# Attention maxima of two heads in one VectorE operation, and eight PSUM banks shared out anew

## The chip, the cores and the metric

The kernel runs on one core of a Trainium2 chip. The metric is the device time of one execution in microseconds, the median of several. The core has five engines: TensorE (PE), VectorE (DVE), ScalarE (ACT), GpSimd (POOL) and SyncE (SP, which here only issues DMAs). PSUM holds 8 banks of 512 float32 columns for each of 128 partitions; PE writes its results there.

## The reference

Four blocks run one after the other on `x` of 16 batches x 128 tokens x 256 channels, each adding its output times a gate: a recurrence over time (WKV), a gated feed-forward network, an attention with 16 heads of 8 dimensions, and a mixture of 8 experts with a shared one. The change lies in the attention. In it, x of one batch is read as 128 channels x 256 positions:

```python
q = einsum('oc,bct->bot', Wq, target) + bq      # target: layernorm(x), source: the context
k = einsum('oc,bcs->bos', Wk, source) + bk
v = einsum('oc,bcs->bos', Wv, source) + bv
dot = einsum('bhdt,bhds->bhts', q, k) / sqrt(8)         # 16 heads, 256 x 256 scores each
dot = mask * dot - (1.0 - mask) * 1e6
amap = softmax(dot, axis=-1) * mask
out = einsum('bhts,bhds->bhdt', amap, v)
```

The inputs make scores large, so the softmax needs the maximum of each row.

## The kernel before, in words

The attention stage takes from about 155 to 387 us. Each head's scores are computed twice. First straight (line 1126, `score`): 256 positions t as two halves of 128 partitions by 256 positions s, which fills one bank; DVE takes the maximum over s (line 1259), two numbers a partition. The maxima of all 16 heads go through a transpose on PE (1213), a negation on ACT (1289), a split into three bf16 parts on POOL and a round trip through DRAM into rows of `QKA`, the operand of the scores. Then the scores are computed a second time, turned (line 1141, `score_T`): s on the partitions, t on the columns, two heads to a bank, with the negated maximum already in the sum. ACT takes the exponential of such a bank (1308), and PE multiplies with the values (1225, PV, four column groups of 32), accumulating in bank 6.

The loop over batches (`turns`) has 8 slots a batch, the same for each engine. In slot p of batch b PE does the scores of heads pair p of batch b+2 and the turned scores of slot p of batch b, woven together (`pe_both`): for each of two halves n, one straight matmul, one turned, one straight, one turned; the two kinds use different rows of the array where they can. Then it does the PV of the slot two before. In slot 0 the PV of the previous batch and the maxima's transpose follow; in slot 1 another PV comes first, and after it ACT copies bank 6 out (1313); PE turns the result in slots 3 (1234) and 5 (1241), and projects a later batch in slot 6 (633). DVE does two reductions a slot, and in slots 3, 4 and 5 a reciprocal (1267), the division (1274) and the addition to x (1282). ACT does two exponentials a slot, the copy in slot 1, and now and then a piece of another batch's projection (652, 662). 14 of 16 batches have both kinds of scores in the loop; the last two have only turned ones (`pe_scoresT`, `act_tail_exp`, the tail), and the first two batches' straight scores are done before the loop (`pe_scores`).

Each engine executes its instructions in order. Semaphores tie them: `a_s` counts banks of scores filled, `a_red` banks reduced, `a_st` turned banks filled, `a_exp` exponentials done. Straight scores use banks 0, 1, 2 by turns and turned ones 3, 4, 5. `score_bank` makes PE wait until the bank's last user has been reduced, and `turned_bank` until the exponential has read the bank; with three banks that is three heads, or three exponentials, back. The 16th head uses bank 1 (4 for turned scores) so that every batch starts alike. Banks 6 and 7 hold the values' sums and small transposes.

Of the kernel before, what the change touches and what calls it, by code (L numbers as in the profile page):

```python
# [8 lines left out]
ALU = mybir.AluOpType  # L9
ACT = mybir.ActivationFunctionType  # L10
AX = mybir.AxisListType
# [39 lines left out]
def flamingo_kernel(nc, x, ctx, mask, g_xattn, g_ffn, time_decay, time_first, gate_wT, up_wT, down_wT,  # L51
# [11 lines left out]
    with ExitStack() as keep:  # L63
# [161 lines left out]
        with ExitStack() as part:  # L225
# [135 lines left out]
            def later(count):  # L361

                return not isinstance(count, int) or count > 0
# [263 lines left out]
            def at(g, k, ahead):  # L627

                return g + (k + ahead) // GB, (k + ahead) % GB
# [433 lines left out]
            with ExitStack() as att:  # L1063
# [36 lines left out]
                a_mg = semp("a_mg")  # L1100

                SBK = [bank[0], bank[1]]
                THIRDS = [n % 3 for n in range(HEADS - 1)] + [1]
                SBK3, TBK3 = bank[0:3], bank[3:6]

                def last_use(n):

                    return max(m for m in range(-HEADS, n) if THIRDS[m % HEADS] == THIRDS[n])
                PVB, MISC = bank[6], bank[7]

                PT = HP[:, :, :].rearrange("p (a s q) (r t) -> p a s (q r) t", a=2, s=2, r=2)
# [25 lines left out]
                def score_T(pe, k, q, st, m, to=None):  # L1137
                    rows, h = rows_of(turned_head(q, m))
                    if to is None:
                        to = TBK3[THIRDS[turned_at(q, st, m // 2)]]  # L1140
                    return pe.matmul(to[:, (m % 2) * T:(m % 2 + 1) * T], QKA[rows, k, 1, h, st * P:(st + 1) * P],  # L1141
                                     QKA[rows, k, 0, h, :], start=True, stop=True)

                def turned_at(i, st, half):

                    return 2 * (2 * i + st) + 1 - half
# [6 lines left out]
                def score_bank(pe, g, k, n):  # L1153

                    score_filled(pe, g, k, n)
                    pe.wait_ge(a_red, HEADS * (GB * g + k) + last_use(n) + 1)

                def turned_bank(pe, g, k, i, st, half):

                    b, m = GB * g + k, turned_at(i, st, half)  # L1160
                    if m == 0:
                        pe.wait_ge(a_mx[k], 32 * (g + 1))
                    if later(HEADS * b + last_use(m) + 1):
                        pe.wait_ge(a_exp, HEADS * b + last_use(m) + 1)

                def pe_scores(pe, g, k, p, SBK):

# [28 lines left out]
                def pe_both(pe, to_score, to_turn, p):  # L1196


                    i, st = p // 2, p % 2
                    for n, half in ((2 * p, 1), (2 * p + 1, 0)):  # L1200
                        to = SBK3[THIRDS[n]]
                        if first(GB * to_turn[0] + to_turn[1]) and p == 0:
                            pe.wait_ge(s_x2, 1 + 2 * G3 + n + 1)
                        score_bank(pe, *to_score, n)
                        score(pe, to_score[1], n, 0, to)
                        turned_bank(pe, *to_turn, i, st, half)
                        score_T(pe, to_turn[1], i, st, 2 * half)
                        score(pe, to_score[1], n, 1, to).then_inc(a_s, 1)
                        score_T(pe, to_turn[1], i, st, 2 * half + 1).then_inc(a_st, 1)
# [40 lines left out]
                    pch.wait()  # L1250
                    pool.tensor_tensor(Z3[:], Z3[:], rstd3[:, bass.ds(b, 1)].broadcast_to([P, T]), ALU.mult).then_inc(a_z3, 1)

                def dve_reduce(dve, g, k, n, SBK=None):
                    b, par = GB * g + k, k % 2
                    if n == 0 and later(b - 1):
                        dve.wait_ge(a_mxT, b - 1)
                    dve.wait_ge(a_s, HEADS * b + n + 1)
                    src = SBK[(HEADS * b + n) % 3] if SBK else SBK3[THIRDS[n]]
                    dve.tensor_reduce(MX[:, par, head_of(n), :], src[:, :].rearrange("p (a s) -> p a s", a=2),  # L1259
                                      axis=AX.X, op=ALU.max).then_inc(a_red, 1)  # L1260

                yt = MISC[:, :].rearrange("p (x r) -> p x r", r=2 * HD)

# [36 lines left out]
                def act_exp(act, g, k, i, st):  # L1300
                    b = GB * g + k
                    n = 8 * b + 2 * i + st
                    for half in (1, 0):
                        m = turned_at(i, st, half)
                        act.wait_ge(a_st, HEADS * b + m + 1)
                        if half == 1 and later(n - 3):
                            act.wait_ge(a_pv, n - 3)
                        act.activation(PT[:, i % 2, st, 2 * half:2 * half + 2, :].rearrange("p j t -> p (j t)"),  # L1308
                                       TBK3[THIRDS[m]], ACT.Exp).then_inc(a_exp, 1)

                def act_av(act, b):
                    act.wait_ge(a_pv, 8 * b + 8)
# [82 lines left out]
                def there(b, ahead=0):  # L1395

                    return not isinstance(b, int) or 0 <= b + ahead < B
# [31 lines left out]
                with nc.Block() as block:  # L1429
# [199 lines left out]
                    @block.vector  # L1629
                    def _(dve):  # L1630
                        fch = Chain(dve, s_dvech, after_wkv[0])
                        ln4 = Chain(dve, m_ln)
                        ch = Chain(dve, a_dve)
                        ln3 = Chain(dve, s_ln3, after_ln3[0])

                        def reduces(b, lo, hi):
                            for h in range(lo, hi):
                                dve_reduce(dve, 0, b, h, PRO)

                        for i in range(NI):  # L1640
                            if i > 1:
                                reduces(0, 4 * (i - 2), 4 * (i - 2) + 2)
                            dve_h1(dve, fch, G3, i)
                            dve_h(dve, fch, G3, i)
                            if i > 1:
                                reduces(0, 4 * (i - 2) + 2, 4 * (i - 2) + 4)
                            if i == 0:
                                dve_z3(dve, AHEAD_V)
                                dve.tensor_scalar(maskG[:, :, :], maskT[:, :, :], tg[:, 1:2], None, ALU.mult).then_inc(a_mg, 1)
                            if i == 1:  # L1650
                                dve_stats3(dve, ln3, 2)
                        dve_z3(dve, AHEAD_Q)
                        reduces(1, 0, 16)
                        dve_x2(dve, G3, DB)
                        dve.wait_ge(a_mg, 1)

                        def slot(ch, g, k, p):
                            b = GB * g + k
                            if there(b, AHEAD_S):
                                dve_reduce(dve, *at(g, k, AHEAD_S), 2 * p)  # L1660
                            if there(b, AHEAD_S):
                                dve_reduce(dve, *at(g, k, AHEAD_S), 2 * p + 1)
                            if isinstance(b, int) and 8 * b + p in LAST_STATS:
                                dve_one_of_last(dve, ln3, LAST_STATS.index(8 * b + p))
                            if p == 3 and there(b, -1):
                                dve_sums(dve, ch, b - 1)
                            if p == 4 and there(b, -1):
                                dve_y(dve, ch, b - 1)
                            if p == 5 and there(b, -1):
                                dve_x3(dve, b - 1)  # L1670
                            for t in STAT4.get(tail(b, p), ()):
                                dve_statistics(ln4, tiles_of(t))
                            for t in NORM4.get(tail(b, p), ()):
                                dve_normalise(dve, tiles_of(t), t + 1)
                            if tail(b, p) == MOST4:
                                dve.wait_ge(a_x3, B - 1)
                                alone(dve)
                                dve_statistics(ln4, OTHERS)
                            if tail(b, p) == MOST4 + 1:
                                dve_normalise(dve, OTHERS, NG)  # L1680
                            if tail(b, p) == MOST4 + 2:
                                hidden_shared(Chain(dve, m_dve), 0, 0)
                            if tail(b, p) == MOST4 + 5:
                                dve.wait_ge(a_x3, B)
                                alone(dve)
                                dve_statistics(ln4, LAST)
                            if tail(b, p) in range(TURN4, TURN4 + 2 * G3):
                                dve_turn4(dve, *divmod(tail(b, p) - TURN4, 2), SBK[(tail(b, p) - TURN4) % 2])

                        turns(dve, slot, ch, a_dve, 1)  # L1690
# [477 lines left out]
```

## Time and profile before

| | us |
|---|---|
| median of 3 runs (lowest, highest) | 521.47 (521.08, 521.91) |
| the profiled execution | 522.43 |
| its span, first to last instruction | 520.7 |
| busy in the span: PE, DVE, ACT, POOL | 473.5, 379.4, 243.7, 229.9 |
| mean granted clock of PE | 0.996 |

The profile comes from one execution. PE's matmuls overlap, so its busy time is no measure of its work. L1259 is line 1259 of the kernel. "Idle before" is the time in which an engine stood still ahead of an instruction, with the instruction or DMA that released it; a wait for several things is put down to the last of them.

### The profile page before, as it was taken

What the parts mean: (1) busy time and instruction counts of PE and PEld (TensorE: products, weight loads), DVE (VectorE), ACT (ScalarE), POOL (GpSimd) and SP (SyncE); (2) the same over time, 40 slices, a digit from 0 to 9 for tenths busy, and PEclk for the clock granted to TensorE, in tenths of its full rate; (3) what the DMA queues carried; (4) which work ended last, traced back from release to release, by engine and by line L of the source; (5) the groups of instructions that cost most, each with busy time, mean ns of one, the idle gap of its engine ahead of it and who ended that gap; (6) DMA issues with size and microseconds to landing.
All of it is one profiled execution on the core that took longest, in us unless ns stands there. A gap on an engine that the chain in (4) does not pass through costs nothing. (4 is left out here: it accounts for less than half of the span.)

```text
span 520.7 us, 10383 instructions
## 1 busy us (share of the span) xinstructions
PE 473.5 (91%) x3384; PEld 259.2 (50%) x3384; DVE 379.4 (73%) x770; ACT 243.7 (47%) x461; POOL 229.9 (44%) x304
## 2 busy tenths in 40 slices
PE   2988999998989889999899999998999999999993
PEld 2653564753733533334334334333434746788882
DVE  4989879789668989999888999999645734333331
ACT  2742223221222068888788888878611001133331
POOL 3673224143438447666667667413010470042433
PEclk9999999999999999999999999999999999999998
DMA  7655800000255536556576565620004124468753
GB/s 241 204 167 124 147 18 0 1 1 1 62 144 146 137 88 172 138 145 166 144 198 158 151 174 152 153 47 6 3 4 162 52 102 156 132 155 211 185 116 40
DMA packets 67255, 59.95 MB, mean 115 GB/s; under 512 B 10048, under 2 KB 62256, under 8 KB 67216
## 3 DMA queue, kind: packets, MB, share of 16 engines
q1 hardware_dynamic: 63712, 55.24, 39.1%
q0 software_dynamic: 3072, 4.21, 4.8%
q8 instruction: 22, 0.36, 0.3%
q14 instruction: 17, 0.14, 0.1%
q10 hardware_dynamic: 432, 0.00, 0.0%
HBM read 38.90 MB, written 22.50 MB: 118 GB/s over the span
## 5 line engine op out<-in xcount | busy, mean ns | idle before, releaser
L1259 DVE TENSOR_REDUCE MX<-psum 128x2 f32<-128x512 f32 x256 | 161.2, 683 | 17.1 <-PE psum L1126 16.4
L1308 ACT ACTIVATE HP<-psum 128x512 f32<-128x512 f32 x224 | 120.8, 603 | 29.1 <-PE psum L1141 27.5
L1126 PE MATMUL psum<-QKA 60*128 60x256 bf16 x512 | 79.7, 273 | 14.4 <-DVE MX L1259 9.8
L1225 PE MATMUL psum<-HP,VP 128*32 128x256 f32 x1024 | 81.8, 391 | 0.2 <-issue 0.2
L1141 PE MATMUL psum<-QKA 60*128 60x256 bf16 x512 | 78.8, 273 | 2.1 <-DMA QKA<-max_scr 1.6
L566 PE MATMUL psum<-space_a,space_w 128*128 128x512 f32 x160 | 72.6, 600 | 3.5 <-DVE HP L593 2.1
L1126 PEld LDWEIGHTS psum<-QKA 60*128 60x128 bf16 x512 | 33.0, 94 | 70.5 <-DVE MX L1259 53.0
L1848 POOL DMA_INDIRECT out_x<-OE,to_u x16 | 25.0, 1564 | 62.3 <-ACT OE L1883 59.9
L579 ACT ACTIVATE space_a<-psum,hgs 128x512 f32<-128x512 f32 (+1 forms) x24 | 15.6, 650 | 72.0 <-PE psum L566 46.4
L566 PEld LDWEIGHTS psum<-space_a,space_w 128*128 128x128 f32 x160 | 29.0, 190 | 39.4 <-issue 32.3
L1971 PE MATMUL psum<-XT,WE 128*128 128x256 f32 (+1 forms) x192 | 44.0, 379 | 0.9 <-ACT XT L1867 0.9
L199 PE MATMUL psum<-space_a,wsh 128*128 128x512 f32 (+1 forms) x96 | 43.6, 598 | 0.3 <-PEq L1429 0.3
L606 PE MATMUL psum<-space_w,HP 128*128 128x256 f32 x160 | 37.9, 385 | 0.0
L1971 PEld LDWEIGHTS psum<-XT,WE 128*128 128x128 f32 (+1 forms) x192 | 34.3, 181 | 7.3 <-issue 1.1
L1141 PEld LDWEIGHTS psum<-QKA 60*128 60x128 bf16 x512 | 30.7, 94 | 7.8 <-issue 3.8
L1225 PEld LDWEIGHTS psum<-HP,VP 128*32 128x32 f32 x1024 | 20.2, 108 | 27.0 <-issue 15.4
L606 PEld LDWEIGHTS psum<-space_w,HP 128*128 128x128 f32 x160 | 29.4, 190 | 5.9 <-issue 2.4
L2119 DVE SCALAR_TENSOR_TENSOR KR<-KR,psum 128x256 f32<-128x256 f32 (+1 forms) x24 | 10.1, 420 | 30.0 <-ACT KR L1874 30.0
L684 POOL TENSOR_TENSOR QK<-QK,PARTS 128x512 f32<-128x512 f32 x16 | 18.5, 1159 | 20.2 <-ACT PARTS L662 20.2
L199 PEld LDWEIGHTS psum<-space_a,wsh 128*128 128x128 f32 (+1 forms) x96 | 16.6, 181 | 21.2 <-issue 21.1
L465 DVE RECIPROCAL DEN<-DEN 128x512 f32<-128x512 f32 x8 | 26.6, 3338 | 0.0
L1874 ACT ACTIVATE KR<-psum 128x256 f32<-128x256 f32 (+1 forms) x24 | 9.2, 383 | 36.8 <-PE psum L1971 36.8
(191 smaller groups left out, 737.6 us busy)
## 6 DMA issues: line engine op xcount, KB each, us to landing
QKA<-stack_scr SPq DMA_DIRECT2D x32, 480.0 KB, 4.7
stack_scr<-PARTS SPq DMA_DIRECT2D x32, 192.0 KB, 2.6
WE<-in_W SPq DMA_DIRECT2D x16, 352.0 KB
stack_scr<-PARTS SPq DMA_DIRECT2D x32, 128.0 KB, 2.1
XD<-dispatched SPq DMA_DIRECT2D x8, 258.0 KB, 3.8
X<-in_x SPq DMA_DIRECT2D x4, 512.0 KB, 5.7
CTX<-in_ctx SPq DMA_DIRECT2D x4, 512.0 KB, 7.9
MB<-in_mask SPq DMA_DIRECT2D x16, 128.0 KB, 3.1
```

The costliest lines, as they stand in the source:

```text
L199: last = pe.matmul(bank[2 * i + side][0:m, :], (wsh1, wsh3)[side][:, h, i * P:i * P + m], ZT4[:, h, bass.ds(GT * g, GT)], start=(h == 0), ...
L465: dve.reciprocal(DEN[:, h, :], DEN[:, h, :]).then_inc(s_rec, 1)
L566: last = pe.matmul(to[:, :], w[:, h, i * P:(i + 1) * P], ZT[:, h, :], start=(h == 0), stop=(h == 1))
L606: pe.matmul(to[f], HP[:, i, t * P:(t + 1) * P], dw[:, i, :], start=(i == 0), stop=False)
L684: pool.tensor_tensor(QK2 if r == 0 else part_of(2), QK2, part_of(r), ALU.subtract).then_inc(a_rest, 1)
L1126: return pe.matmul(to[:, tt * T:(tt + 1) * T], QKA[rows, k, 0, h, tt * P:(tt + 1) * P], QKA[rows, k, 1, h, :], start=True, stop=True)
L1141: return pe.matmul(to[:, (m % 2) * T:(m % 2 + 1) * T], QKA[rows, k, 1, h, st * P:(st + 1) * P], QKA[rows, k, 0, h, :], start=True, stop=True)
L1225: last = pe.matmul(PVB[32 * j:32 * j + 32, (m // 2) * T:(m // 2 + 1) * T], VP[:, k, st, turned_head(i, m), :], PT[:, i % 2, st, m, :], sta ...
L1259: dve.tensor_reduce(MX[:, par, head_of(n), :], src[:, :].rearrange("p (a s) -> p a s", a=2), axis=AX.X, op=ALU.max).then_inc(a_red, 1)
L1308: act.activation(PT[:, i % 2, st, 2 * half:2 * half + 2, :].rearrange("p j t -> p (j t)"), TBK3[THIRDS[m]], ACT.Exp).then_inc(a_exp, 1)
L1848: pool.indirect_dma_start(out=out_rows, out_offset=bass.IndirectOffsetOnAxis(ap=to_u[:, e, a:a + 1], axis=0), in_=OE[:, s, a, :], in_offse ...
L1971: last = pe.matmul(bank[i][0:m, lo:lo + CAP], w[:, s, h, i * P:i * P + m], XT[:, s, h, :], start=(h == 0), stop=(h == 1))
```

## The change

The two reductions of a slot become one over two neighbouring banks, 1,024 columns, which writes the maxima of both heads and adds 2 to `a_red`. It waits until both banks are filled. Straight scores now use four banks, 0 to 3, two a slot; PE waits once per slot, for the pair of two slots before. Turned scores use two banks, 4 and 5, by turns, so PE waits for the exponential two before the one that the bank is for. The stage ahead of the loop and the tail are as they were.

```diff
--- before.py
+++ after.py
@@ -1100,12 +1100,7 @@
                 a_mg = semp("a_mg")
 
                 SBK = [bank[0], bank[1]]
-                THIRDS = [n % 3 for n in range(HEADS - 1)] + [1]
-                SBK3, TBK3 = bank[0:3], bank[3:6]
-
-                def last_use(n):
-
-                    return max(m for m in range(-HEADS, n) if THIRDS[m % HEADS] == THIRDS[n])
+                SBK4, TBK2 = bank[0:4], bank[4:6]
                 PVB, MISC = bank[6], bank[7]
 
                 PT = HP[:, :, :].rearrange("p (a s q) (r t) -> p a s (q r) t", a=2, s=2, r=2)
@@ -1137,7 +1132,7 @@
                 def score_T(pe, k, q, st, m, to=None):
                     rows, h = rows_of(turned_head(q, m))
                     if to is None:
-                        to = TBK3[THIRDS[turned_at(q, st, m // 2)]]
+                        to = TBK2[turned_at(q, st, m // 2) % 2]
                     return pe.matmul(to[:, (m % 2) * T:(m % 2 + 1) * T], QKA[rows, k, 1, h, st * P:(st + 1) * P],
                                      QKA[rows, k, 0, h, :], start=True, stop=True)
 
@@ -1153,15 +1148,16 @@
                 def score_bank(pe, g, k, n):
 
                     score_filled(pe, g, k, n)
-                    pe.wait_ge(a_red, HEADS * (GB * g + k) + last_use(n) + 1)
+                    if n % 2 == 0:
+                        pe.wait_ge(a_red, HEADS * (GB * g + k) + n - 2)
 
                 def turned_bank(pe, g, k, i, st, half):
 
                     b, m = GB * g + k, turned_at(i, st, half)
                     if m == 0:
                         pe.wait_ge(a_mx[k], 32 * (g + 1))
-                    if later(HEADS * b + last_use(m) + 1):
-                        pe.wait_ge(a_exp, HEADS * b + last_use(m) + 1)
+                    if later(HEADS * b + m - 1):
+                        pe.wait_ge(a_exp, HEADS * b + m - 1)
 
                 def pe_scores(pe, g, k, p, SBK):
 
@@ -1198,7 +1194,7 @@
 
                     i, st = p // 2, p % 2
                     for n, half in ((2 * p, 1), (2 * p + 1, 0)):
-                        to = SBK3[THIRDS[n]]
+                        to = SBK4[n % 4]
                         if first(GB * to_turn[0] + to_turn[1]) and p == 0:
                             pe.wait_ge(s_x2, 1 + 2 * G3 + n + 1)
                         score_bank(pe, *to_score, n)
@@ -1250,14 +1246,24 @@
                     pch.wait()
                     pool.tensor_tensor(Z3[:], Z3[:], rstd3[:, bass.ds(b, 1)].broadcast_to([P, T]), ALU.mult).then_inc(a_z3, 1)
 
-                def dve_reduce(dve, g, k, n, SBK=None):
+                def dve_reduce(dve, g, k, n, SBK):
                     b, par = GB * g + k, k % 2
                     if n == 0 and later(b - 1):
                         dve.wait_ge(a_mxT, b - 1)
                     dve.wait_ge(a_s, HEADS * b + n + 1)
-                    src = SBK[(HEADS * b + n) % 3] if SBK else SBK3[THIRDS[n]]
+                    src = SBK[(HEADS * b + n) % 3]
                     dve.tensor_reduce(MX[:, par, head_of(n), :], src[:, :].rearrange("p (a s) -> p a s", a=2),
                                       axis=AX.X, op=ALU.max).then_inc(a_red, 1)
+
+                def dve_reduce_pair(dve, g, k, p):
+                    b, par = GB * g + k, k % 2
+                    if p == 0:
+                        dve.wait_ge(a_mxT, b - 1)
+                    dve.wait_ge(a_s, HEADS * b + 2 * p + 2)
+                    lo = 2 * (p % 2) * 512
+                    dve.tensor_reduce(MX[:, par, p:p + HALF + 1:HALF, :],
+                                      psum[:, lo:lo + 1024].rearrange("p (h a s) -> p h a s", h=2, a=2),
+                                      axis=AX.X, op=ALU.max).then_inc(a_red, 2)
 
                 yt = MISC[:, :].rearrange("p (x r) -> p x r", r=2 * HD)
 
@@ -1306,7 +1312,7 @@
                         if half == 1 and later(n - 3):
                             act.wait_ge(a_pv, n - 3)
                         act.activation(PT[:, i % 2, st, 2 * half:2 * half + 2, :].rearrange("p j t -> p (j t)"),
-                                       TBK3[THIRDS[m]], ACT.Exp).then_inc(a_exp, 1)
+                                       TBK2[m % 2], ACT.Exp).then_inc(a_exp, 1)
 
                 def act_av(act, b):
                     act.wait_ge(a_pv, 8 * b + 8)
@@ -1657,9 +1663,7 @@
                         def slot(ch, g, k, p):
                             b = GB * g + k
                             if there(b, AHEAD_S):
-                                dve_reduce(dve, *at(g, k, AHEAD_S), 2 * p)
-                            if there(b, AHEAD_S):
-                                dve_reduce(dve, *at(g, k, AHEAD_S), 2 * p + 1)
+                                dve_reduce_pair(dve, *at(g, k, AHEAD_S), p)
                             if isinstance(b, int) and 8 * b + p in LAST_STATS:
                                 dve_one_of_last(dve, ln3, LAST_STATS.index(8 * b + p))
                             if p == 3 and there(b, -1):
```

## Rows read from the trace of the kernel before

**Rows 1.** Costliest groups of the page: busy us, mean ns | idle before, releaser (times).

```profile
L1259 DVE TENSOR_REDUCE MX<-psum 128x2 f32<-128x512 f32 x256 | 161.2, 683 | 17.1 <-PE psum L1126 16.4
...
L1308 ACT ACTIVATE HP<-psum 128x512 f32<-128x512 f32 x224 | 120.8, 603 | 29.1 <-PE psum L1141 27.5
...
L1126 PEld LDWEIGHTS psum<-QKA 60*128 60x128 bf16 x512 | 33.0, 94 | 70.5 <-DVE MX L1259 53.0
```

**Rows 2.** Table of waits from 199 to 357: us in total, times, longest.

```profile
PEld psum L1141 <- ACT HP L1297: 0.4, 1, 0.4
```

**Rows 3.** One batch: length; busy PE, PEld, DVE, ACT, POOL; granted clock; DMA share, GB/s.

```profile
306.92:318.75 11.83, 11.34 (x142) 4.51 (x139) 10.96 (x21) 10.42 (x22) 8.09 (x13) 1.00 0.66 174
```

**Rows 4.** Timeline in order of time, ACT: start us, us, instruction, [idle before <-releaser].

```profile
309.11 0.60 ACT L1313 ACTIVATE AV<-psum 128x512 f32<-128x512 f32 x1 [0.33 <-PE psum L1225]
...
309.61 2.06 ACT L1308 ACTIVATE HP<-psum 128x512 f32<-128x512 f32 x4
...
311.52 0.66 ACT L662 ACTIVATE PARTS<-QK 128x512 bf16<-128x512 f32 x1
...
313.38 1.09 ACT L1308 ACTIVATE HP<-psum 128x512 f32<-128x512 f32 x2 [0.23 <-PE psum L1141]
```

**Rows 5.** The same timeline, PE (PEld: weight loads).

```profile
308.19 0.28 PE L1213 MATMUL psum<-ident,MX 128*32 128x128 f32 x1
...
308.41 0.64 PE L1225 MATMUL psum<-HP,VP 128*32 128x256 f32 x8
...
308.98 0.28 PE L1126 MATMUL psum<-QKA 60*128 60x256 bf16 x1
...
310.15 0.09 PEld L1126 LDWEIGHTS psum<-QKA 60*128 60x128 bf16 x1 [0.62 <-DVE MX L1259]
...
310.57 0.64 PE L1225 MATMUL psum<-HP,VP 128*32 128x256 f32 x8
...
312.26 0.65 PE L1234 MATMUL psum<-ident,AV 128*128 128x128 f32 x4
...
312.97 0.37 PE L1141 MATMUL psum<-QKA 60*128 60x256 bf16 x2
...
315.13 0.44 PE L1241 MATMUL psum<-ident,YA 128*128 128x128 f32 x2
...
315.50 0.28 PE L1141 MATMUL psum<-QKA 60*128 60x256 bf16 x1
...
316.05 0.64 PE L1225 MATMUL psum<-HP,VP 128*32 128x256 f32 x8
...
316.73 0.69 PE L633 MATMUL psum<-Z,wq 128*128 128x256 f32 x2
...
317.36 0.28 PE L1126 MATMUL psum<-QKA 60*128 60x256 bf16 x1
```

**Rows 6.** The same, DVE, and one small reduction at 398 us.

```profile
309.40 3.68 DVE L1259 TENSOR_REDUCE MX<-psum 128x2 f32<-128x512 f32 x6 [0.77 <-PE psum L1126]
...
313.00 0.35 DVE L1267 RECIPROCAL RD<-psum 128x32 f32<-128x32 f32 x1
...
398.26 0.29 DVE L2026 TENSOR_REDUCE mxl<-L 128x16 f32<-128x128 f32 x1
```

**Rows 7.** Timeline, the tail's exponentials and PE's wait on one.

```profile
356.73 2.85 ACT L1297 ACTIVATE HP<-psum 128x1024 f32<-128x1024 f32 x3
...
357.80 0.12 PEld L1141 LDWEIGHTS psum<-QKA 60*128 60x128 bf16 x4 [0.71 <-ACT HP L1297]
```

**Rows 8.** Timeline, ACT's copies of the values, three of the 16.

```profile
199.40 0.60 ACT L1313 ACTIVATE AV<-psum 128x512 f32<-128x512 f32 x1 [0.33 <-PE psum L1225]
...
320.94 0.60 ACT L1313 ACTIVATE AV<-psum 128x512 f32<-128x512 f32 x1 [0.33 <-PE psum L1225]
...
356.24 0.60 ACT L1313 ACTIVATE AV<-psum 128x512 f32<-128x512 f32 x1
```

**Rows 9.** Timeline, a matmul of scores that waited for a DMA.

```profile
258.39 0.28 PE L1126 MATMUL psum<-QKA 60*128 60x256 bf16 x1 [0.86 <-DMA QKA<-stack_scr]
```

## What is predicted, before the changed kernel was run

> **What bounds the kernel now.** The costliest groups of the page come first [rows 1]: the maxima, 256 reductions of 161 us on DVE, and the exponentials, 224 of 121 us on ACT, both inside the attention loop. The weight loads of the scores' matmuls sat idle 53 us until DVE had freed a bank. In the table of waits, cut to the loop, the turned scores' matmuls have one wait on ACT, of 0.4 us, and that on L1297, the tail's [rows 2]. So three turned banks are enough for ACT today, and the three score banks are what stops PE. A batch of the loop takes 11.83 us, with DVE busy 10.96 and ACT 10.42 [rows 3]: both nearly full, ACT half a microsecond behind. The busy share of PE says little, since its matmuls overlap; their starts say more.
>
> So I read one batch, 306.92 to 318.75, start by start [rows 4 to 6]. PE's own work in a slot, without waits: the turned matmuls start in four steps 0.11 apart, the values' matmuls (PV) start about 0.53 after the first (315.50 to 316.05 is 0.55 with its rounding), and take 0.57 to the next thing (308.41 to 308.98): 1.10. Besides, once per batch: 0.22 for the maxima's transpose (308.19 to 308.41), 0.59 for L1234 (312.26 to 312.85, one step ahead of 312.97), 0.37 for L1241 (315.13 to 315.50), 0.73 for L633 with the gap before it (PV's end 316.62 to 317.36). Slots 1 and 2 follow each other without a PV, 0.44 for 0.53. 8 x 1.10 + 1.91 - 0.09 = 10.62. The other 1.21 of the 11.83 are waits; the largest is in slot 2, on DVE: PV starts there 1.59 after slot 1 (308.98 to 310.57) where 0.44 + 0.53 = 0.97 would do, so 0.62 [rows 5]. DVE idles 0.77 in slot 1, and then runs on [rows 6].
>
> **The change, part by part.** *Two reductions of 512 become one of 1,024*, in 14 batches x 8 slots = 112. Six back to back take 3.68 and one lasts 0.68, so they start 0.60 apart, 1.20 for a pair [rows 6]. A reduction of 128 elements lasts 0.29, one of 512 0.68 [rows 6]: 1.02 ns an element. The long one should last 0.68 + 0.52 = 1.20 and let the next start after 0.60 + 0.52 = 1.12: 0.08 saved. The ends: 0.15 saved, if only elements cost (1,024 x 1.02 ns = 1.05), and 0.08 lost, if the halves do not overlap at all (0.60 + 0.68 = 1.28). I take 0.08, as the slope is of the same operation. DVE's batch falls from 10.96 to 10.3.
>
> *The pair starts later*: it needs both heads, the second 0.22 after the first, so a DVE that waits restarts that much later. *Four score banks instead of three*: a slot now needs the pair of two slots back, whose banks are free some 1.25 after its start, itself 0.31 after that slot's last score. In the schedule below this stops PE nowhere. The counts that SP's fills and POOL's values wait for (L1363, L1329) keep their values and come with PE.
>
> *Two turned banks instead of three.* The matmul of turned bank m waits for exponential m-2 instead of m-3. It stands on PE's queue ahead of the second score of its head, the next head, and PV, so whatever it waits, DVE waits too. The trace has no such wait; its parts it has:
> a) with ACT free, an exponential starts 0.41 after the second turned matmul of its bank (312.97 to 313.38) [rows 4, 5];
> b) exponentials follow each other by (2.06 - 0.60)/3 = 0.49 [rows 4];
> c) in the tail one started at 356.73, lasted 1.02 (of three, 2.85 together), and PE's wait on it ended at 357.80, 0.05 after its end [rows 7]. So a bank is free 0.60 + 0.05, say 0.66, after its exponential's start;
> d) in slot 1 ACT first copies the values, 0.70 after the PV ahead of slot 1 started (308.41 to 309.11), and starts exponential 2 0.50 after that (309.61).
>
> Slot 2, counted from that PV: exponential 3 starts at 0.70 + 0.50 + 0.49 = 1.69, its bank is free at 2.35, slot 2's last matmul starts one step later at 2.46, the next PV at 2.66. Without waits this PV would start at 0.57 + 0.97 = 1.54, and it starts today at 2.16. The wait is 1.12 where the one on DVE was 0.62: 0.50 more.
>
> A slot that directly follows one in which ACT was empty: the exponentials start 0.52 and 1.01 after the first slot's start, the second bank is free at 1.67, and PE wants it at 1.10 + 0.22 = 1.32: a wait of 0.35. This strikes slots 5 and 0. Slots 4, 6, 7 and 1 have L1234, L1241, L633, and the transpose with the extra PV ahead of them, which cover it, but for 0.03 in slot 6; in slot 3, behind slot 2's long wait, 0.08 are left. ACT's other work (L662, L652, the negation) fits between. Waits: 1.12 + 0.08 + 0.35 + 0.03 + 0.35 = 1.93, and a batch 10.62 + 1.93 = 12.55, which is 0.72 more. With 10.3 of work in it DVE has 2 us to spare, so the price of the long reduction, anywhere between its ends, changes nothing.
>
> On grouping, the Trainium skill (Perfetto Trace Analysis, Optimizing Scalar/DVE Operations) says that a DVE operation on PSUM carries about 125 ns of overhead and that larger operations help where the engine is saturated; by that the estimated saving is 112 x 0.125 = 14 us, where the slope gives 9. The same section says that an engine that isn't saturated but makes others idle is better served by smaller pieces. No run here shows either yet; the second speaks against the change.
>
> **Sum.** The copies of the values start once per batch, 16 in all, among them at 199.40, 320.94 and 356.24 [rows 8]. The ten batches to 320.94 take 121.54; at 12.55 they take 125.5: +4.0. In one of them PE stood 0.86 in slot 0 for a DMA [rows 9], and more behind it; if the slower pace doesn't absorb such waits it is up to 1.6 more. I take +4.8. The three batches to 356.24 take 11.77 today; they have no L633 (-0.73), which uncovers slot 7 (0.35) and leaves 0.08 of slot 0's: 10.62 - 0.73 + 1.93 + 0.35 - 0.27 = 11.91, +0.14 each, +0.4. The loop's first batch, which copies no values, ends 0.4 later by the same walk (ACT starts empty, and the slots follow each other closely). Together +5.6. The tail and what follows are as before, and PE passes the delay on. The profiled execution took 522.43 with a span of 520.7, and the median of the runs is 521.47: 528.0 in the terms of the one, 527.1 in the other's.
>
> **The rivals.** 1, the other side: *turned banks come free before PE asks, and DVE's gain arrives.* What is left are waits on the pairs: 0.37 in slot 3 (pair 1 starts 0.64 after slot 1 does, its banks are free at 1.89 + 0.02, PE asks at 0.44 + 1.10 = 1.54) and some 0.29 ahead of L1241. 10.62 + 0.66 = 11.28, 0.55 less in 13 batches: -7, 514.3. For it: 53 us of waits on DVE and none on L1308 [rows 1, 2]. Against it: exponential 2 ended at 310.21 [rows 4], and PE would ask for its bank at 308.98 + 0.44 = 309.42. It decides where slot 2's wait stays under 0.1.
> 2: *the new waits fall into the old ones.* With 0.62 in slot 2 as today and 0.2 in slots 5 and 0, a batch takes 10.62 + 0.62 + 0.4 + 0.1 = 11.74: 521. For it: the waits of today are in the same slots. Against it: the chain in slot 2 would have to be 0.5 shorter, and each of its parts stands in a row.
> 3: *a reduction over two banks is dear.* DVE binds again where 8 of them and the other 10.96 - 9.60 = 1.36 fill 12.55, from 1.40 each. At 1.5 a batch is 13.4, 0.8 more in 13: 537. No row points to it.
>
> **Chances.** Forecast 0.60, rival 1 0.22, rival 2 0.12, rival 3 0.06. A measurement of this kernel tells 0.2%, 1 us, from nothing. Rival 2 spreads over that line, with 0.01 of it counted slower: faster 0.22, same 0.11, slower 0.67. If the batch's 0.72 is off by 0.3 either way the forecast alone is 523 to 530; for eight in ten it must take in part of rival 1: 516.5 to 530.
>
> **What the changed profile would show.** Right: weight loads of L1141 wait for L1308, 12 us or more, most of it in slot 2; the wait of L1126 on DVE under 15; copies of the values 12.5 apart; 112 reductions of 1.20, DVE busy some 9 less, and idle over 12 more in the loop. Wrong: copies 11.3 apart (rival 1), or a DVE without gaps at over 1.4 a reduction (rival 3). If the PV of slot 2 starts much before 2.66 after the PV ahead of slot 1, one of a to d is off.

## The result, and the profile after

| us | before | after |
|---|---|---|
| median | 521.28 (520.63 to 521.91) | 527.5 (526.84 to 527.56) |
| ratio, 95% interval | | 1.0116 (1.0095 to 1.0137) |
| the profiled execution | 522.43 | 527.45 |
| its span | 520.7 | 525.4 |
| DVE busy in the span | 379.4 | 376.3 |

One further execution of the changed kernel took 564.74 us at a granted clock of 0.851 and is left out of the range and the ratio; the median of the other three is 527.45. The forecast was 527.1. The costliest groups of the page after (the columns are those of [rows 1]; lines of the kernel have moved by a few, 1141 is now 1136, 1126 is 1121, 1225 is 1221, 1308 is 1314, 1313 is 1319):

```profile
L1264 DVE TENSOR_REDUCE MX<-psum 128x4 f32<-128x1024 f32 x112 | 136.1, 1220 | 21.8 <-PE psum L1121 20.7
...
L1314 ACT ACTIVATE HP<-psum 128x512 f32<-128x512 f32 x224 | 121.6, 598 | 33.1 <-PE psum L1136 32.4
...
L1136 PE MATMUL psum<-QKA 60*128 60x256 bf16 x512 | 82.3, 275 | 9.4 <-ACT HP L1314 7.3
...
L1121 PEld LDWEIGHTS psum<-QKA 60*128 60x128 bf16 x512 | 37.7, 94 | 48.0 <-issue 29.3
...
L1136 PEld LDWEIGHTS psum<-QKA 60*128 60x128 bf16 x512 | 30.4, 94 | 30.1 <-ACT HP L1314 22.0
```

The 112 long reductions last 1.22 each. The waits have changed places: the scores' weight loads waited 53 us for DVE before [rows 1], and now L1136, the turned scores, waits 22.0 for the exponentials by the row of the loads. The 7.3 of the matmuls' row are parts of the same stops, seen by the matmul instead of its weight load, and are not added. The table of waits of the loop alone, 199 to 364 us, says the same; before, L1141 had 0.4 there, on the tail's L1297 [rows 2]:

```profile
PEld psum L1136 <- ACT HP L1314: 20.9, 51, 0.8
...
DVE MX L1264 <- PE psum L1121: 19.0, 50, 0.8
...
PE psum L1136 <- ACT HP L1314: 7.3, 13, 0.6
...
PEld psum L1121 <- DVE MX L1264: 5.6, 13, 0.7
```

One batch of the changed kernel, in the timeline, with the PV ahead of slot 1 at its head (x2 or x4 behind an instruction means that so many follow each other in one row):

```profile
299.78 0.64 PE L1221 MATMUL psum<-HP,VP 128*32 128x256 f32 x8
...
300.49 0.60 ACT L1319 ACTIVATE AV<-psum 128x512 f32<-128x512 f32 x1 [0.33 <-PE psum L1221]
...
300.98 2.23 ACT L1314 ACTIVATE HP<-psum 128x512 f32<-128x512 f32 x4
...
301.07 1.23 DVE L1264 TENSOR_REDUCE MX<-psum 128x4 f32<-128x1024 f32 x1 [0.65 <-PE psum L1121]
...
301.62 0.09 PEld L1136 LDWEIGHTS psum<-QKA 60*128 60x128 bf16 x1 [0.84 <-ACT HP L1314]
...
302.12 0.09 PEld L1136 LDWEIGHTS psum<-QKA 60*128 60x128 bf16 x1 [0.27 <-ACT HP L1314]
...
302.44 0.64 PE L1221 MATMUL psum<-HP,VP 128*32 128x256 f32 x8
...
302.51 2.44 DVE L1264 TENSOR_REDUCE MX<-psum 128x4 f32<-128x1024 f32 x2 [0.22 <-PE psum L1121]
...
303.35 0.27 PE L1121 MATMUL psum<-QKA 60*128 60x256 bf16 x1
...
305.46 1.22 DVE L1264 TENSOR_REDUCE MX<-psum 128x4 f32<-128x1024 f32 x1 [0.25 <-PE psum L1121]
...
306.42 0.09 PEld L1136 LDWEIGHTS psum<-QKA 60*128 60x128 bf16 x1 [0.27 <-ACT HP L1314]
...
306.61 0.60 DVE L1280 SCALAR_TENSOR_TENSOR YA<-psum,maskG,RD 128x128 f32<-128x128 f32 x2
...
311.11 0.09 PEld L1136 LDWEIGHTS psum<-QKA 60*128 60x128 bf16 x1 [0.27 <-ACT HP L1314]
```

PV at 299.78, the copy of the values 0.71 later, exponential 2 1.20 later; slot 2's turned scores get their banks at 301.62 and 302.12, and the next PV starts at 302.44, which is 2.66 after the first. Before it was 2.16 [rows 5]. The waits at 306.42 and 311.11 are those of slots 5 and 0. DVE stands 0.65 ahead of slot 1's pair and 0.22 and 0.25 ahead of two later ones, where no idle time of over 0.15, the least that a row shows, stood between slot 1 and slot 7 before [rows 6]. The batch as a whole (columns as in [rows 3]) and three copies of the values [rows 8]:

```profile
300.35:312.79 12.44, 11.88 (x142) 5.02 (x139) 10.77 (x13) 10.44 (x21) 8.02 (x14) 1.00 0.59 157
```

```profile
200.30 0.60 ACT L1319 ACTIVATE AV<-psum 128x512 f32<-128x512 f32 x1 [0.33 <-PE psum L1221]
...
325.36 0.60 ACT L1319 ACTIVATE AV<-psum 128x512 f32<-128x512 f32 x1 [0.33 <-PE psum L1221]
...
361.05 0.60 ACT L1319 ACTIVATE AV<-psum 128x512 f32<-128x512 f32 x1
```

The steady batch takes 12.44 where it took 11.83, at nearly the same work of ACT (10.44) and slightly less busy time of DVE (10.77, 10.96 before). From copy to copy, ten batches take 125.06 (121.54 before), the three after them 35.69 (35.30), and the first copy comes 0.90 later: 4.81 together, and the span grew by 4.7. The medians differ by more, 6.2, since the profiled execution of the kernel before was 1.15 slower than its median and that of the changed kernel was not.

### The profile page after: what moved, and what is told of

It reads as the page before. It is cut to its first block and busy times, and to the rows that moved or that the text cites. A ratio compares the mean times of both kernels' runs of the same rounds, so it can differ in the third digit from the quotient of the medians.

```text
span 525.4 us, 10281 instructions
## 1 busy us (share of the span) xinstructions
PE 480.9 (92%) x3384; PEld 264.9 (50%) x3384; DVE 376.3 (72%) x658; ACT 244.1 (46%) x461; POOL 230.3 (44%) x304
## 5 line engine op out<-in xcount | busy, mean ns | idle before, releaser
L1264 DVE TENSOR_REDUCE MX<-psum 128x4 f32<-128x1024 f32 x112 | 136.1, 1220 | 21.8 <-PE psum L1121 20.7
L1136 PE MATMUL psum<-QKA 60*128 60x256 bf16 x512 | 82.3, 275 | 9.4 <-ACT HP L1314 7.3
L1121 PE MATMUL psum<-QKA 60*128 60x256 bf16 x512 | 85.2, 275 | 4.5 <-DVE MX L1255 1.5
L1121 PEld LDWEIGHTS psum<-QKA 60*128 60x128 bf16 x512 | 37.7, 94 | 48.0 <-issue 29.3
L1136 PEld LDWEIGHTS psum<-QKA 60*128 60x128 bf16 x512 | 30.4, 94 | 30.1 <-ACT HP L1314 22.0
```

The lines of the kernel that those rows point to most:

```text
L1121: return pe.matmul(to[:, tt * T:(tt + 1) * T], QKA[rows, k, 0, h, tt * P:(tt + 1) * P], QKA[rows, k, 1, h, :], start=True, stop=True)
L1264: dve.tensor_reduce(MX[:, par, p:p + HALF + 1:HALF, :], psum[:, lo:lo + 1024].rearrange("p (h a s) -> p h a s", h=2, a=2), axis=AX.X, op=A ...
```

## Experiments

Twelve more variants of the same loop (orders, bank shares, shortened exponentials) were timed, each in several executions against the kernel before on the same chip. The kernel before took 520.87 beside e1 to e4, 521.25 beside e5 to e8, 521.57 beside e9 to e11 and 523.17 beside e12, so runs of different groups are compared by their ratios. "Batch" is the steady distance of the copies of the values in each trace, 11.8 before and 12.44 after. The code excerpts are shortened.

| run | score/turned banks, reduction | us | ratio to before, 95% | batch |
|---|---|---|---|---|
| e1 | 4/2, single | 525.7 | 1.0099 (1.0079 to 1.0118) | 12.44 |
| e2 | 3/2, single | 527.99 | 1.0136 (1.0119 to 1.0153) | 12.53 |
| e3 | 4/2, long, half exponentials | 521.42 | 1.0002 (0.9982 to 1.0023) | 11.61 |
| e4 | 3/3, single, half exponentials | 522.23 | 1.0018 (1.0000 to 1.0037) | 11.8 |
| e5 | 4/2, long, PV behind slot 1 | 534.44 | 1.0245 (1.0206 to 1.0284) | 13.0 |
| e6 | 4/2, long, PV between halves | 534.01 | 1.0239 (1.0202 to 1.0277) | 12.9 |
| e7 | 3/3, single, PV between halves | 520.91 | 0.9985 (0.9969 to 1.0002) | 11.87 |
| e8 | 4/2, single, PV between halves | 524.36 | 1.0060 (1.0042 to 1.0078) | 12.17 |
| e9 | 4/2, long, PV and copy behind slot 1 | 522.12 | 1.0000 (0.9974 to 1.0026) | 12.10 |
| e10 | 3/3, single, PV behind, copy between | 520.82 | 0.9973 (0.9949 to 0.9997) | 11.75 |
| e11 | 4/2, long, copy behind | 529.2 | 1.0131 (1.0073 to 1.0190) | 12.66 |
| e12 | as e9, half exponentials | 520.5 | 0.9952 (0.9924 to 0.9980) | 11.3 to 11.6 |

### e1 and e2: the two parts apart

```diff
 # e1, against the changed kernel: two reductions, four score banks, two turned banks
-    if n % 2 == 0: pe.wait_ge(a_red, HEADS * (GB * g + k) + n - 2)      # PE's queue
+    pe.wait_ge(a_red, HEADS * (GB * g + k) + n - 3)
-    dve.wait_ge(a_s, HEADS * b + 2 * p + 2)
-    dve.tensor_reduce(MX[:, par, p:p + HALF + 1:HALF, :], psum[:, lo:lo + 1024]...).then_inc(a_red, 2)
+    dve.wait_ge(a_s, HEADS * b + n + 1)
+    dve.tensor_reduce(MX[:, par, head_of(n), :], SBK4[n % 4]...).then_inc(a_red, 1)
```

> The changed kernel with only the pairing undone: two reductions of 512 columns a slot again, each with its own wait, over the same four score banks and two turned banks. Theory (the loss is the wait for the second turned bank): PE's waits on ACT stay, 1.9 us a batch; DVE's work is back at 11.0 a batch, still under the 12.44 that a batch takes, so the time stays at 527.5, within 1. Rival (the pair's coarser start and release is what costs): the time falls back to about 521.5.

```diff
 # e2, against the kernel before: only the turned banks
-SBK3, TBK3 = bank[0:3], bank[3:6]
+SBK3, TBK2 = bank[0:3], bank[4:6]
-        pe.wait_ge(a_exp, HEADS * b + last_use(m) + 1)
+        pe.wait_ge(a_exp, HEADS * b + m - 1)
```

> The kernel before with one part of the change alone: two turned banks instead of three. Three score banks and single reductions as before. Theory: slot 2 stands 1.12 us on ACT instead of 0.62 on DVE, slots 5 and 0 0.35 each, so 527 to 529 (up to 1 over the changed kernel, as three score banks can add a wait on DVE). Rival (turned banks are not the cause): 521.5, no change.

Waits of the loop (199 to 362) in e1, and then in e2:

```profile
PEld psum L1136 <- ACT HP L1311: 20.8, 52, 0.8
...
PEld psum L1121 <- DVE MX L1262: 21.5, 66, 0.4
```

```profile
PEld psum L1126 <- DVE MX L1259: 32.3, 95, 0.9
...
PEld psum L1141 <- ACT HP L1308: 17.9, 39, 0.8
```

e1 gives the old reductions back and its steady batch is still 12.44, the same to the hundredth as with the long one. e2 takes only the third turned bank away and loses all that the change loses: its 527.99 lies in the 527 to 529 expected. So the loss comes from the missing third turned bank, and the rival of a coarse pair is out for the steady batch. It is not out for the whole time. e1 was expected within 1 of 527.5 and took 525.7, 1.8 less. In the traces its first copy is 0.67 earlier (199.63), most likely because the loop's first reduction can start on one bank, and most of the rest comes in the next two batches (24.63 together against 25.57). The ratios to the kernel before, 1.0099 and 1.0116, do not tell the two apart.

### e3 and e4: ACT made faster

```diff
-    act.activation(PT[:, i % 2, st, 2 * half:2 * half + 2, :]..., TBK2[m % 2], ACT.Exp)
+    act.activation(PT[:, i % 2, st, 2 * half, :], TBK2[m % 2][:, 0:T], ACT.Exp)
```

> The changed kernel with half of each exponential in the loop left out (256 of 512 columns, the values' matmuls read the computed half twice), so that ACT frees turned banks about 0.2 us sooner each. Theory: PE's waits on ACT fall from 1.9 us a batch to under 0.4, and a batch comes to 11.0 to 11.4, about 1.1 less in 13 batches: 511 to 515. Rival (DVE's long reduction or its later start sets the pace): 525 to 528.

> The kernel before with the same half of each exponential left out. Theory: with three turned banks nothing waited for ACT, and DVE sets the pace, so 521 within 1; the gap between this and the changed kernel with half exponentials, 6 to 10 us, is what the pairing is worth where turned banks come free in time. Rival (ACT was a bound of the old kernel too): 518 or less.

With exponentials of 0.38 instead of 0.60 the changed kernel's batch falls from 12.44 to 11.61, and the old kernel's stays at 11.8. The waits of L1136's loads for exponentials are down to 8.0 us (22.0 in the changed kernel), and ACT was no bound before: e4 gained nothing (522.23, a little above the 520 to 522 expected). But 521.4 is not 511 to 515. Three things were left out of that expectation. Slot 2's chain loses only the two exponentials' difference, so that 0.62 of idle time of the loads is left there. L1237, which waits for the division behind slot 4's pair, stands 0.70, where it stood 0.41 in the changed kernel. And two batches took 12.87 and 13.01, in which PE's matmuls waited 1.09 for a DMA, and 0.41 and 0.66. The steady batches of e3 and e4 differ by 0.2, not by the 0.5 or more expected; that is the worth of pairing and of the fourth score bank less that of the third turned one, as all three differ. The two ratios do not tell e3 from e4.

### e5, e11, e9: which instruction starts the chain

```diff
 # e5, PE's queue (e9 too)
-    if p == 1: pe_pv(pe, *at(g, k, -1), 3, st)
     pe_both(pe, at(g, k, AHEAD_S), (g, k), p)
+    if p == 1: pe_pv(pe, *at(g, k, -1), 3, st)
 # e11, ACT's queue (e9 too)
-    if p == 1: act_av(act, b - 1)
     act_exp(act, g, k, p // 2, p % 2)
+    if p == 1: act_av(act, b - 1)
```

> The changed kernel with one instruction group moved: the PV that stood ahead of slot 1 stands behind it, so that slots 1 and 2 no longer follow each other without a PV. Theory: the wait on ACT in slot 2 falls from 1.12 to 0.35 us, slot 1 gets one of 0.13: 0.64 less a batch, 13 batches, 8.3 less: 519, within 1.5. Rival (ACT's copy of the values, not the closeness of the slots, makes the wait): the copy moves back with its PV and the wait stays, 527 to 529.

> The changed kernel with ACT's copy alone moved, behind both exponentials of slot 1; the PV stays ahead of slot 1. Theory by the walk of the prediction: exponentials 2 and 3 start at 1.09 and 1.58 after that PV instead of 1.20 and 1.69, so slot 2's scores come 0.11 sooner, but its PV then waits for the copy (done at 2.67, the PV at 2.72 instead of 2.66) and slot 3's second turned bank is 0.1 later still: 12.5 to 12.7 a batch, 528 to 531. Rival (the copy's place ahead of exponential 2 is most of the 1.12 us wait in slot 2): 520 or less.

e5 was expected at 519 and took 534.4, above the rival's 527 to 529 too. Its timeline, slots 1 and 2:

```profile
291.43 0.28 PE L1121 MATMUL psum<-QKA 60*128 60x256 bf16 x1
...
291.99 0.64 PE L1221 MATMUL psum<-HP,VP 128*32 128x256 f32 x8
...
292.69 0.60 ACT L1319 ACTIVATE AV<-psum 128x512 f32<-128x512 f32 x1 [0.81 <-PE psum L1221]
...
293.19 2.23 ACT L1314 ACTIVATE HP<-psum 128x512 f32<-128x512 f32 x4
...
293.83 0.09 PEld L1136 LDWEIGHTS psum<-QKA 60*128 60x128 bf16 x1 [1.18 <-ACT HP L1314]
```

Slot 1's scores are done from 291.43 on, but the copy of the values stands ahead of exponential 2 on ACT's queue, and waits for the moved PV (0.81 idle). So exponential 2 starts 1.76 after slot 1 instead of 0.63 (300.98 less 300.35), and PE loses 1.18 at the next bank. That the copy moves back with its PV, as the rival's sentence has it, is what happened, at a higher price than the rival gave: 13.0 a batch. e11 moves the copy alone:

```profile
288.54 0.64 PE L1221 MATMUL psum<-HP,VP 128*32 128x256 f32 x8
...
289.65 1.08 ACT L1314 ACTIVATE HP<-psum 128x512 f32<-128x512 f32 x2 [0.66 <-PE psum L1136]
...
290.30 0.09 PEld L1136 LDWEIGHTS psum<-QKA 60*128 60x128 bf16 x1 [0.75 <-ACT HP L1314]
...
290.62 0.60 ACT L1319 ACTIVATE AV<-psum 128x512 f32<-128x512 f32 x1
...
291.32 0.64 PE L1221 MATMUL psum<-HP,VP 128*32 128x256 f32 x8
```

Exponential 2 starts 1.11 after the PV (1.09 expected), the bank is had at 1.76, the next PV starts at 2.78 (2.72 expected), and the time of 529.2 lies in the range given. So the copy's place alone is not the cause of the wait of 1.12 either: with the copy moved away the bank comes 0.08 sooner (1.76, 1.84 in the changed kernel), and the next PV 0.12 later, and the batch is 0.22 longer. e9 moves both:

> As the run with the PV moved behind slot 1 over four score and two turned banks with the long reduction, and ACT's copy of the values also moved, behind both exponentials of slot 1. In the earlier run the copy stood ahead of the exponentials on ACT's queue and held them until the moved PV was done (13.0 us a batch). Theory (the turned banks' chain starts with whatever stands ahead of the exponentials): exponentials 2 and 3 now start 0.52 and 1.01 after slot 1, slot 2 waits 0.35 on ACT and some 0.17 for the copy ahead of its PV; a batch comes to 12.0 to 12.3, that is 522 to 526. Rival (the closeness of slots 1 and 2 never mattered): 527 or more.

```profile
296.05 1.08 ACT L1314 ACTIVATE HP<-psum 128x512 f32<-128x512 f32 x2 [0.17 <-PE psum L1136]
...
297.02 0.60 ACT L1319 ACTIVATE AV<-psum 128x512 f32<-128x512 f32 x1
...
297.19 0.09 PEld L1136 LDWEIGHTS psum<-QKA 60*128 60x128 bf16 x1 [0.27 <-ACT HP L1314]
...
297.72 0.64 PE L1221 MATMUL psum<-HP,VP 128*32 128x256 f32 x8
```

Here slot 2's second bank (297.19) costs the same 0.27 as in slots 0 and 5, and the batch is 12.10, within the 12.0 to 12.3 expected. What made slot 2 dear was slots 1 and 2 back to back with a queue on ACT ahead of them: neither e5 nor e11, which move one of the two, takes the wait away, and e9, which moves both, does. 522.1 is a draw with the kernel before, so nearly all of the change's loss is won back by the order, with two turned banks still.

### e6, e7, e8: PV between the halves of a slot

```diff
     for n, half in ((2 * p, 1), (2 * p + 1, 0)):
...
         score_T(pe, to_turn[1], i, st, 2 * half + 1).then_inc(a_st, 1)
+        if half == 1 and between:
+            between()          # the slot's PV; on ACT the copy goes between the two exponentials
```

> The changed kernel with each slot's PV between its two halves, and ACT's copy between the two exponentials of slot 1: turned banks are asked for at even distances of about 0.55 us, while ACT takes 0.49 each. Theory: nearly all of the 1.93 us of waits a batch go, PE's own 10.62 and a few tenths remain, 10.9 to 11.2 a batch: 508 to 514, the upper end if DMA waits as in the half-exponential run (three batches of 12.1 to 13.0) come back. Rival (DVE's long reduction and its later start then bind at 11.8 or more): 519 or more.

> The kernel before (three and three banks, single reductions) with the same order, PV between the halves. Theory: DVE's own 10.96 us a batch is the floor and its idle time in slot 1 (0.77) mostly goes: 11.1 to 11.3 a batch, 513 to 516. Rival (DVE's waits stay): 519 to 522.

> As the last but one, PV between the halves over four score and two turned banks, but with two single reductions a slot instead of the long one. Theory: the difference to the kernel with the long reduction is what pairing is worth where turned banks come in time: DVE-bound at 10.96 or more a batch here, 0 to 0.3 us a batch slower, so 0 to 4 us over it. Rival (the pair's late start costs more than it saves): this one is the faster, by up to 3 us.

All three missed the theory's number. e6 (508 to 514 expected) is the slowest but one. In its timeline (slot 4's pair, the division, PE's L1239):

```profile
296.55 1.22 DVE L1266 TENSOR_REDUCE MX<-psum 128x4 f32<-128x1024 f32 x1 [0.32 <-PE psum L1121]
...
297.69 0.60 DVE L1282 SCALAR_TENSOR_TENSOR YA<-psum,maskG,RD 128x128 f32<-128x128 f32 x2
...
298.34 0.20 PEld L1239 LDWEIGHTS psum<-ident,YA 128*128 128x128 f32 x2 [0.99 <-DVE YA L1282]
```

Even spacing serves ACT: in the loop no load of L1136 waits over 0.15 for it (20.9 us in the changed kernel). But a pair is complete only with the second half, which now comes after the PV, so the pair starts late, the division YA behind it is late, and L1239's loads stand 0.99 for it (0.41 in the changed kernel). e8, the same order with single reductions, is 9.6 us faster than e6, where its theory had it up to 4 slower and its rival up to 3 faster: the first head's reduction uses the time that the pair spends waiting. Here the pairing costs 0.7 a batch. e7 (513 to 516 expected) left the old kernel as it was, at 11.87 a batch, as its rival said.

### e10 and e12: the floors

> The kernel before, three and three banks and single reductions, with the PV behind slot 1 and ACT's copy between the exponentials of slot 1. Theory: DVE restarts 0.57 sooner after slot 0, its idle 0.77 in slot 1 falls to 0.1 to 0.2, three turned banks give the copy room, and a batch comes to 11.1 to 11.4 where it took 11.8: 513 to 518, the upper end if DMA waits come back. Rival (PE's waits move elsewhere, or the copy holds the PV of slot 2 up): 520 to 522.

In e10 DVE's idle time in slot 1 is gone, as meant, but the batch is 11.75 and not 11.1 to 11.4. The timeline of DVE, and below it one reduction of the eight by itself, with the last matmul of its scores:

```profile
282.19 2.56 DVE L1259 TENSOR_REDUCE MX<-psum 128x2 f32<-128x512 f32 x4
...
285.03 5.22 DVE L1259 TENSOR_REDUCE MX<-psum 128x2 f32<-128x512 f32 x8 [0.28 <-PE psum L1126]
...
286.15 0.27 PE L1126 MATMUL psum<-QKA 60*128 60x256 bf16 x1
...
286.45 0.69 DVE L1259 TENSOR_REDUCE MX<-psum 128x2 f32<-128x512 f32 x1
```

By (5.22 - 0.68)/7 the eight start 0.65 apart, and it looks as if DVE ran without a stop, at a slower pace than the 0.60 of [rows 6]. It did not: one row takes in instructions with less than 0.15 of idle time between them. Five of the seven distances are 0.60 or 0.61; the other two are 0.81 (to 286.45, right behind its scores, which end at 286.42) and 0.71, both waits for PE. Sixteen reductions 0.60 apart and the small operations of a batch (0.27, 0.52 for two and 0.33, by the starts of the instructions behind them in the kernel before), fill 10.7 of the 11.75; the rest is waiting. So the idle time of slot 1 has moved to other slots, which is what the rival said, and e10 is no floor of DVE's. One batch of 15.7 (235.97 to 251.69) contains a DMA wait of 2.1 of PE's; the profiled execution took 523.5, the longest of the ten. The median is 0.27% under the kernel before, with 0.03% left at the end of the interval, and it has the lowest ratio of those that leave nothing out; e7's interval overlaps it.

> The changed kernel with the PV behind slot 1, ACT's copy behind both exponentials of slot 1, and half of each exponential in the loop left out (256 of 512 columns, the values' matmuls read the computed half twice). Theory: now no turned bank makes PE wait (a bank is free 0.43 us after its exponential's start, exponentials 0.27 apart), what is left are about 0.3 us of waits around the copy and L1237's wait on DVE, and a steady batch comes to 10.9 to 11.1; DVE at 10.3 of work keeps up only thanks to the long reduction. With DMA waits in three batches, as in the other half-exponential run, 510 to 515. Rival (the long reduction's late start binds at 11.6 as in the first half-exponential run): 518 to 521.

e12 has 3.3 us of waits of L1136's loads on ACT in the whole loop, so the turned banks are out of the way, and DVE has slack. Six of its first ten batches take 11.3 to 11.6, three 11.8 to 11.9 and one 14.2; the eleventh takes 13.4. In the 14.2, what stopped PE and POOL; then PE's wait for the division in an undisturbed batch, and two long reductions in a row:

```profile
246.35 0.28 PE L1121 MATMUL psum<-QKA 60*128 60x256 bf16 x1 [1.51 <-DMA QKA<-stack_scr]
...
247.74 0.73 POOL L670 TENSOR_TENSOR QK<-KR,MB 128x256 f32<-128x256 f32 x1 [3.68 <-DMA MB<-in_mask]
...
301.17 0.44 PE L1237 MATMUL psum<-ident,YA 128*128 128x128 f32 x2 [0.22 <-DVE YA L1280]
...
315.60 2.37 DVE L1264 TENSOR_REDUCE MX<-psum 128x4 f32<-128x1024 f32 x2 [0.34 <-PE psum L1121]
```

The operands go through DRAM, with DMAs issued by SP. PE's stops for them in the loop, each counted once, come to 5.5 us in e12 and 2.2 in the kernel before. Over all runs they go with the pace: 1.5 to 5.5 where the steady batch is 11.9 or less (the kernel before, e3, e4, e7, e10, e12), at most 0.6 where it is 12.1 or more (the changed kernel and the other seven). Which part of that path is slow no run here separates. The other stop that stays in every batch of e12 is the division behind the late pair: L1237's loads stand 0.70 for it, as in e3. So with ACT at half its work little of the long reduction's gain arrives: 0.5% under the 523.17 of the kernel before beside it, where 510 to 515 had been expected against some 521.

## Why the prediction was right

- **The bound.** The prediction had PE waiting for score banks and not for ACT. e4 (ACT faster, nothing gained) shows the second. That DVE alone sets the pace is more than the runs show: its operations fill 10.7 of a batch of 11.8 by their starts, PE's own work 10.6 by the prediction's sum, and the two wait for each other; moving DVE's idle time (e7, e10) gave 0.3% at most.
- **The wait in slot 2.** Forecast: the PV of slot 2 2.66 after the first, 0.50 more than before. Measured: 2.66, and 0.50. Terms b to d hold one by one in the rows above: the copy at 0.71, exponential 2 at 1.20, its bank at 1.84, the next one's at 2.34. Term a) stands too: slot 4's exponential starts 0.42 after the second turned matmul of its bank (304.87 to 305.29).
- **The waits of 0.35 in slots 5 and 0.** They are there, 306.42 and 311.11, with 0.27 idle of the weight loads; slots 5 and 0 start at 305.86 and 310.55, and 0.22 later their second halves would, so each is 0.34 late.
- **The batch.** Forecast 12.55, measured 12.44, 0.1 too much; ten batches 125.5 against 125.06. The three after them come to 35.69 against 35.7 by luck: they take 11.62, 11.75 and 12.31, and not 11.91 each (the terms as written give 11.90). The first batch was taken too cheaply: 0.4 forecast, 0.90 measured, 0.67 of it against e1, which differs in the pair alone; the walk did not follow the pair's later start there.
- **DMA waits absorbed.** The ten batches cost 3.5 where +4.8 was taken: 0.4 of the difference is the 0.1 a batch, and 0.8 was a reserve for DMA waits that was not needed. PE's stops for DMAs fell to 0.5 in the loop.
- **The number.** The sum was +5.6 and the trace has +4.8, so the errors cancel only in part. That the median, 527.5, came out 0.4 from the forecast 527.1 is partly luck of the executions: the medians differ by 6.2. In the terms of the profiled execution 528.0 was forecast and 527.45 measured.
- **Which part does it.** Named: two turned banks, with the long reduction without effect on the steady batch. e1 and e2 show both.
- **A term mis-sized.** The long reduction was to save 0.08 a pair and 9 us of DVE's busy time. It lasts 1.22 and lets the next operation start 1.14 after its own start, be it a small one (305.46 to 306.61) or, in e12, another long one; 1.12 was forecast. That is 0.06 saved against two singles 0.60 apart. The two in a row at 302.51 take 2.44 because the second waited for its scores, which end at 303.62, 0.11 before it starts. In e12 two in a row take 2.37 (315.60), so that they start 1.14 to 1.15 apart. DVE's busy time fell by less than the saving: 140.9 us between the first and fourteenth copy, and 145.4 in e1 over the same 13 batches, 4.5 in 104 pairs, 0.04 each (3.1 in the whole span). A record is 0.08 longer than the distance to a next one that follows at once, and where a gap follows, as behind most long reductions, those 0.08 count as busy. DVE idles 6.8 more in the loop, and not "over 12". By the Trainium skill (Perfetto Trace Analysis, Optimizing Scalar/DVE Operations) it would have been some 0.125 a pair; the durations do differ by 2 x 0.68 - 1.22 = 0.14, but single ones overlap, and the measurement decides. The advice of the Trainium skill in the same section, to break up operations where they make others idle, is borne out by e8 against e6.
- **A claim on the profile.** "Most of it in slot 2" holds: 0.84 + 0.27 of the 1.65 that the loads of L1136 stand in the batch shown. The wait on DVE is under 15, as said (5.6 in the loop).
- **The rivals.** Rival 1 was priced too well. Its 514.3 took for granted that nothing else stands behind ACT. e12, where the turned banks don't bind, has 11.3 to 11.6 with another order of the PV, and DMA waits, not 11.28 and none; its stop for the division is the 0.29 that rival 1 named (0.70 less the 0.41 of an ordinary slot). Rival 2 is out: the PV of slot 2 came 2.66 after the first and not 2.16. Rival 3 is out: 1.22 a reduction, under the 1.40 from which DVE would bind.

The same walk from the rows fared worse on the experiments. e2, e9 and e11 came out in their ranges, and e1 and e4 missed theirs by 0.8 and 0.2. e5 and e6 failed because I moved an instruction and did not follow what was queued behind it: the copy on ACT, the division on DVE. e3, e7, e10 and e12, all expected under 519, came out at 520.5 to 521.4, and e8's difference to e6 had the wrong sign: a wait taken away in one slot came back in another, or as a wait for a DMA. What stays open is why the steady batches with three turned banks do not get below 11.75, when PE has some 10.6 and DVE some 10.7 of work in them.

## What to carry to other kernels

Banks are a budget: a bank given to one consumer is taken from another, and the trace of before can show no wait of the loser at all, only its parts. Add them up (start after the fill, length, release, what else stands in that engine's queue) and compare with when the producer asks again. A longer operation starts when its last input is there; where that is late, two short ones are the better buy. Moving an instruction moves everything that is queued behind it on the engine that waits for it. And a row of the timeline that stands for several instructions can hide short waits: divide its length by their number, and look inside where the distance is not the usual one.

## What the runs showed of the hardware

- A max-reduction on VectorE over two PSUM banks, 1,024 float32 columns, lasts 1.22 us against 0.68 for 512; the slope over columns gives 1.20, so the second bank has no price of its own beyond 0.02. The next operation starts 1.14 after a long one (e12) and 0.60 after one of 512 [rows 6]; the larger distances looked at here (302.51, 285.03) were waits for scores.
- An exponential of 512 PSUM columns lasts 0.60 and one of 256 0.38; the release reaches PE's queue about 0.05 us after the end, in the loop (300.98 + 0.60 to 301.62) as in the tail [rows 7].
